# A four-layer graph network on one core: the cross-product difference of layers 1 and 3 moved from VectorE to GpSimd

## The reference, cut to what matters

```
es = h_s[edge_src]
ev = h_v[edge_src]
m_s1 = w1 * es * e0
m_s2 = w4 * jnp.einsum('eci,ei->ec', ev, e1) * _inv(3)
m_v1 = (w2 * es)[:, :, None] * e1[:, None, :]
m_v2 = w3[:, :, None] * ev * e0[:, :, None]
m_v3 = w5[:, :, None] * jnp.cross(ev, e1[:, None, :]) * _inv(2)
agg_s = jax.ops.segment_sum(mid_s, edge_dst, num_segments=n) * inv_nn
agg_v = jax.ops.segment_sum(mid_v, edge_dst, num_segments=n) * inv_nn
```

## Time and profile before

| what | us |
|---|---|
| three runs | 12054.53, 12107.16, 12102.8 |
| median of the three | 12102.8 |
| the profiled execution, its own time | 12098.74 |
| its span, from the first instruction to the last | 12096.9 |

### The profile page before, as it was taken

One profiled execution on the slowest core, in us unless ns is written; L12 is line 12 of the kernel. 1 busy time (PEld: TensorE's weight loads), 2 busy tenths in 40 slices (PEclk: granted clock), 3 DMA queues, 4 the chain that ended last, 5 costly groups with the idle time before them and its releaser, 6 DMA issues. The chain is left out here.

```text
span 12096.9 us, 245491 instructions
## 1 busy us (share of the span) xinstructions
PE 9397.7 (78%) x46500; PEld 6592.8 (55%) x46501; DVE 9136.3 (76%) x32454; ACT 7003.3 (58%) x26255; POOL 6367.4 (53%) x9502
## 2 busy tenths in 40 slices
PE   4421188888888888888888788887788888788887
PEld 1211177777777777777777344445433335444445
DVE  6702078888888888888887899995565555899996
ACT  0000067777777777777776555553566666676764
POOL 0677646666666666666542455551355553455551
PEclk9855589999999999999998999996799999999997
DMA  6433211111111111111111343333222223343333
GB/s 262 53 66 70 64 31 31 30 30 30 30 31 30 31 30 30 31 30 31 27 17 38 82 87 86 87 85 46 43 53 52 52 52 54 84 87 85 86 85 60
DMA packets 1798441, 691.91 MB, mean 57 GB/s; under 512 B 1586190, under 2 KB 1677258, under 8 KB 1798346
## 3 DMA queue, kind: packets, MB, share of 16 engines
q0 software_dynamic: 219136, 411.56, 14.6%
q1 hardware_dynamic: 1572154, 275.26, 13.5%
q10 hardware_dynamic: 7056, 4.02, 0.1%
HBM read 514.24 MB, written 171.77 MB: 57 GB/s over the span
## 5 line engine op out<-in xcount | busy, mean ns | idle before, releaser
L963 POOL DMA_INDIRECT shared<-table,rec x2640 | 2560.4, 970 | 2508.8 <-issue 1058.4
L1045 PE MATMUL bank<-tp,oh 128*128 128x480 f32 (+1 forms) x5280 | 2407.3, 552 | 6.3 <-DVE tp L1122 4.6
L997 ACT ACTIVATE tp<-tp,rec 128x64 f32<-128x64 f32 x7920 | 2030.3, 335 | 234.1 <-DVE tp L1093 153.2
L1037 PE MATMUL bank<-w_fc,hT 128*128 128x448 f32 x2640 | 1368.5, 601 | 701.5 <-ACT hT L981 447.9
L1680 ACT ACTIVATE shared<-bank 128x512 f32<-128x512 f32 x1760 | 973.6, 595 | 961.9 <-PE bank L1755 955.1
L1045 PEld LDWEIGHTS bank<-tp,oh 128*128 128x128 f32 x5280 | 921.0, 195 | 856.8 <-issue 843.5
L1755 PE MATMUL bank<-ident,tp 128*128 128x128 f32 x7040 | 1054.0, 299 | 265.5 <-ACT tp L813 218.2
L1093 DVE TENSOR_TENSOR tp<-bank,shared 128x256 f32<-128x256 f32 x1320 | 560.2, 424 | 924.3 <-PE bank L1045 613.4
L782 POOL DMA_INDIRECT rec_dst<-ACC x784 | 813.5, 1038 | 602.5 <-issue 571.9
L1755 PEld LDWEIGHTS bank<-ident,tp 128*128 128x128 f32 x7040 | 889.9, 154 | 303.3 <-ACT tp L813 253.6
L1644 POOL DMA_INDIRECT gat<-table,rec x880 | 866.7, 985 | 277.0 <-issue 190.7
(11 more groups left out here) (248 smaller groups left out, 22541.0 us busy)
## 6 DMA issues: line engine op xcount, KB each, us to landing
shared<-table,rec POOLq DMA_INDIRECT x2640
rec_dst<-tp SPq DMA_DIRECT2D x44, 900.0 KB, 23.6
ACC<-in_attrs SPq DMA_DIRECT2D x56, 623.0 KB
rec_src<-tp SPq DMA_DIRECT2D x44, 730.0 KB, 19.9
efr<-rec_src SPq DMA_DIRECT2D x440, 64.0 KB
efr<-rec_dst SPq DMA_DIRECT2D x440, 64.0 KB
ACC<-in_attrs SPq DMA_DIRECT2D x196, 130.0 KB
rec<-rec_dst SPq DMA_DIRECT2D x1320, 10.0 KB
```

The costliest lines, as they stand in the source:

```text
L963: nc.gpsimd.indirect_dma_start(out=gatx[:, u, g, 0:L.row], out_offset=None, in_=tables[L.n][:, :], in_offset=IOff(ap=rec[:, u, g, L.idx:L. ...
L997: done = nc.scalar.activation(t[:, g, lo:lo + 64], t[:, g, 0:64], ACT.Copy, scale=rec[:, u, g, L.y + k:L.y + k + 1])
L1037: nc.tensor.matmul(pW[u % 2][:, 0:448], hT[:, u % 2, :], fc2[:, :], start=True, stop=True)\
L1045: done = nc.tensor.matmul(pS[u % 2][:, 0:TW], oh[:, u, g, :], tp[:, u % 2, g, 64:64 + TW], start=g == 0, stop=g == G - 1)
```

## The change

VectorE no longer computes `cross`. A function `subtract(i, u)` in GpSimd's stream does it: it waits for `vy_ready` of the pair and raises `crossed`. GpSimd's stream is rewritten around it: the gathers of the first four pairs come first; then the loop's body has, for each u, the difference of pair (i, u) and behind it the gathers of pair (i + 1, u); the last four differences follow behind the loop. Layer 2 gets the same loop without the differences. SP, ACT and PE are unchanged, and so are all the waits of `gather` and `records`.

```
-                    with po.Fori(0, QP) as i:
+                    def subtract(i, u):
+                        po.wait_ge(vy_ready.h, vy_ready.done(i, u))
+                        po.sem_inc(pool_tick, 1)
+                        nc.gpsimd.tensor_tensor(cross[:, :, :, :], vy[:, :, 1], vy[:, :, 2], ALU.subtract)\
+                            .then_inc(crossed.h, 1)
+
+                    for u in range(4):
+                        gather(0, u)
+                    with po.Fori(0, QP - 1) as i:
                         for u in range(4):
-                            gather(i, u)
+                            if L.cross:
+                                subtract(i, u)
+                            gather(i + 1, u)
+                    for u in range(4):
+                        if L.cross:
+                            subtract(QP - 1, u)
...
-                        if L.cross:
-                            nc.vector.tensor_tensor(cross[:, :, :, :], vy[:, :, 1], vy[:, :, 2], ALU.subtract).then_inc(crossed.h, 1)
```

## The result

Four runs of the changed kernel take 15,475.91 to 15,491.09 us, median 15,482.22; the kernel before, on the same chip, 12,082.4. The ratio is 1.282, 95% interval 1.279 to 1.284: 3,400 us slower.

What follows compares the result with a forecast made beforehand. PE with its short turn through ScalarE was taken to set 3.40 us a pair, VectorE close behind. Six terms sum to 8.05 us a pair, 436 times a layer: +3920 on 12098.7 gives 16,020 us, range 15,500 to 17,100.

Steps and rivals of the forecast that it cites:

- VectorE's 92%: VectorE's busy share in the edge loops of layers 1 and 3 before the change, 1421.07 of 1550 us.
- the 3.40 us: Length of a good pair in those loops before, start to start of PE's L1037, set by PE and ScalarE.
- The closed ring: Layers 1 and 3: product, record DMAs, gathers, difference, next product wait on each other; 8.05 us a pair against 3.55.
- product's end to gather: First link: L1122 ends, SP issues rec and efr, they land, GpSimd starts the gathers; 4.28 us.
- the subtraction: Fourth link: GpSimd's new 192-column difference, taken as 0.53 us, bounds 0.34 to 0.72.
- GpSimd to VectorE: Fifth link: from GpSimd's end to VectorE's start, in no row; taken as 0.15 us, bounds 0 and 0.31.
- the third link: On GpSimd, from a DMA instruction to an elementwise one; taken as 0.55 us, bounds 0.30 and 0.65.
- Beside the ring: VectorE's other work for a pair, 2.56 us, starting 0.26 us after the previous pair's end; then 4.9 us of waiting.
- Rival A: Chain exists but shorter: first hop only 3.20 us, 6.97 us a pair, 15,077 us; chance 4%.
- PE's clock: Granted clock may fall from 0.99 to 0.50 in the loops; PE's 3.0 us a pair becomes up to 6.0, costing nothing.
- C: No chain, GpSimd the new bound in the loops at 3.87 us a pair, 12,378 us; chance 3%.
- D: Faster: VectorE ready 0.26 us sooner each pair, up to 227 us off, to 11,872 us; chance 3%.

Runs made afterwards that it cites:

- No-difference: Against the kernel before: the difference left out on both engines in layers 1 and 3, with GpSimd's new gather loop; 12,160.25 us, ratio 0.9970.
- Order-only: Against the changed kernel: the difference back on VectorE, GpSimd's new gather loop kept; 12,198.73 us, ratio 1.0016.
- same-work: Against the changed kernel: VectorE computes the difference, GpSimd subtracts 192 columns of still buffers that nobody waits for; 12,144.25 us, ratio 0.9967.
- doubled: Against the changed kernel: each GpSimd subtraction preceded by a second one into a buffer nobody reads; 15,996.91 us, ratio 1.3142.
- between: Against the changed kernel: each difference placed between the two gathers of the pair behind which it stood; 14,465.85 us, ratio 1.1866.
- record-alone: Against the changed kernel: the gathers and VectorE wait for the rec DMA alone, PE for efr, in layers 1 to 3; 14,787.26 us, ratio 1.2132.
- one-ahead: Against the changed kernel: each GpSimd difference one place earlier, pair k+1's ahead of the gathers of pair k+4; 12,513.18 us, ratio 1.0284.
- two-ahead: Against the changed kernel: each GpSimd difference two places earlier; 12,060.04 us, ratio 0.9906 on the first chip, 1.0064 on the third.

## Why the prediction was right and wrong

**What bounds the kernel before: right as far as it was tested.** No-difference shows that VectorE's 92% was no bound: with 0.26 us a pair less, which would be 227 us if VectorE set the pace, 33 came. That PE and its short turn through ScalarE set the 3.40 us fits this, but no run changed PE's work. It was also right that GpSimd's idle time stood behind a wait.

**The closed ring: right in every link.** Order-only and same-work exclude the loop's form and GpSimd's arithmetic; doubled, between and record-alone change three links and find the amount again in the turn; one-ahead spreads the ring over two pairs.

**Its length: wrong, and with it the time.** The forecast was 8.05 us a turn. Medians over the 436 turns of each layer, from the timeline (where two stand, layer 3 and layer 1; the sum takes 4.20 for the first link):

| link | forecast | measured |
|---|---|---|
| product's end to gather | 4.28 | 4.17 to 4.23 |
| two gathers | 2.19 | 2.22 |
| DMA to elementwise on GpSimd | 0.55 | 0.02 |
| the subtraction | 0.53 | 0.60 |
| GpSimd to VectorE | 0.15 | 0.03 |
| last product | 0.35 | 0.35 |
| sum | 8.05 | 7.42 |

The step that failed is the third. I read 0.65 us between a DMA and an elementwise instruction in the earlier trace rows as GpSimd's own cost, though the row names VectorE's L1848 as releaser and I said so. The row that I had not looked up, of the kernel before, is:

```profile
3113.16 0.49 DVE L1848 TENSOR_TENSOR msg<-gat,bank 128x320 f32<-128x320 f32 x1 [0.48 <-issue]
```

L1848 ends at 3113.65, 0.29 us before GpSimd starts: all but this hop was waiting. The link's lower bound, 0.30, was wrong as well, being DMA to DMA; with 0.02 in its place, 15,482 would have been inside the range. This term alone is 0.53 x 872 = 462 us too much, of 537 us by which the profiled difference (3,383) misses the forecast (3,920). The other terms nearly cancel: -0.08, +0.03, +0.07 and -0.12 give -0.10, or 87 us; eight pairs of gathers in each loop that take 4.0 us lift the mean over the median by some 0.04, or 35 us back; and the rest of the program gave 20. With the third link right the forecast would have been 15,560. The turn lies at the edge of the prediction's own last sign of being wrong, a pair under 7.4 us: its median is 7.45 in layer 1 and 7.39 in layer 3.

**Beside the ring:** VectorE stood 3.69 us at its last instruction, not 4.9. Of the 1.2 us, 0.64 are the shorter turn, 0.38 the later start of the next product (0.64 us after the end and not 0.26), and 0.17 its longer work (2.73 us and not 2.56: the forecast took the full 0.35 off for each of two instructions that overlap their neighbours). The shorter turn and the longer work are also why VectorE's busy share is 41% and not 36%. None of this cost time, since it all lay in the wait.

**The subtraction:** 1.66 to 2.2 ns a column gave 0.50 to 0.57 us; it takes 0.595. The Trainium skill's 2.6 cycles an element ("GPSIMD Engine Reference", section 3.1), an estimate of 0.42 us plus dispatch, is compatible with it and would leave 0.17 for the dispatch.

**The landing:** efr's issue to gather is 3.15 us in the median, in a loop that moves 41 GB/s instead of 85. Rival A (3.20 us for the whole hop) is out. The estimate of 2.15 us by the Trainium skill's "DMA: Bandwidth & Descriptors", section "Anatomy of one DMA", which is fitted to the GpSimd path while SP issues efr, doesn't hold here: the trace has 3.15.

**PE's clock:** the granted clock fell as the prediction allowed for, to a mean of 0.74, between the two levels, and cost nothing that shows: PE has 4.6 us of work (1974.25 over 426 pairs) in a turn of 7.46, and VectorE's long wait names GpSimd alone. Two readings beside it were wrong: PE is not idle most of the time but busy 62% (1974.25 of 3184), and the stretch at 0.50 that the prediction calls lightly loaded has PE busy 155.71 of 200 us.

**Rivals C and D** are out: the changed kernel is 28% slower, no-difference leaves at most 0.4% for D, and with the ring opened and the subtraction still on GpSimd a step takes 3.48 to 3.52 us (two-ahead), under the 3.87 of C.

## What to carry to other kernels

An engine's idle time is free only for work whose result isn't needed to end the wait that makes the engine idle. Before moving an instruction into a queue, write down what stands ahead of it, what that waits for, and whether the moved result is on the way to it. If it is, the loop closes and each turn takes the loop's whole length, here 7.4 us instead of 3.55, to save an instruction of 0.26. Each place further forward puts one more pair into the same loop, until something else sets the pace. Before a gap in a row is taken as an engine's cost, look up when the named releaser ended.

## What the runs showed of the hardware that I had not expected

- GpSimd starts an elementwise instruction 0.02 us behind an indirect DMA, but a second indirect DMA 0.30 us behind the first.
- In the changed kernel, where VectorE had to wait at its last instruction of a pair, the next pair's first one started 0.59 us (layer 1) or 0.64 us (layer 3) behind its end in the median. In the kernel before, where it had not waited, the medians are 0.20 and 0.14, and the pair of the earlier trace rows starts 0.09 us ahead of the end. Between them stand a register load and several waits; that they are normally done under the running instruction is my reading, not tested.
- In the changed kernel every 54th pair has 2.12 us between its two gathers instead of 0.30, eight times in each loop, with no releaser named. Why isn't shown.
- The same kernel took 12,082, 12,165, 12,193 and 11,693 us on four occasions, the last three on three different chips, up to 4% apart, and a reordering worth -0.9% on one was +0.6% on another.
